# Swin attention and a spiking layer on one core: keys stored with the four column positions innermost, and ACT's norm of a row split around q's copy

## The reference

```python
x = x + window_attention(group_norm(x))   # 8x8 windows, 16 heads of 16 channels
x = x + spikes(group_norm(x) @ W.T + b)   # 8 samples are the 8 time steps

qkv  = part @ qkv_w.T + qkv_b             # part: 128 windows of 64 tokens
attn = softmax(q * 16**-0.5 @ k.T + bias[h] + MASK[window])
out  = attn @ v
# spikes: v = v + (x_t - v) / 2; s = v >= 1; v = v * (1 - s)
```

## Time and profile before

| | us |
|---|---|
| median of 3 runs | 545.47 |
| lowest, highest | 545.28, 548.49 |
| the profiled execution | 546.64 |
| its span, first to last instruction | 544.9 |
| PE busy | 434.2 (80%) |
| DVE busy | 398.2 (73%) |
| ACT busy | 377.4 (69%) |
| POOL busy | 280.3 (51%) |

### The profile page before, as it was taken

How to read it: one execution, slowest core, us unless ns; L and a number is a source line. 1 busy time by engine, 2 the same in 40 slices (tenths; PEclk the granted TensorE clock), 3 DMA queues, 4 the chain that set the end, 5 groups by cost and what they waited for, 6 DMA issues and landing times.

```text
span 544.9 us, 20474 instructions
## 1 busy us (share of the span) xinstructions
PE 434.2 (80%) x7912; PEld 403.4 (74%) x7912; DVE 398.2 (73%) x838; ACT 377.4 (69%) x863; POOL 280.3 (51%) x382
## 2 busy tenths in 40 slices
PE   0056658889878986988698879889988887889997
PEld 0056558878868886978698779778888776778886
DVE  5753757777776877677767767778877676588897
ACT  2353657878886887678778867788888786756551
POOL 6163456556654766475647654765685556640000
PEclk9996979999998999899989988999999998899999
DMA  7232534556554555455545654565555453023333
GB/s 204 67 81 65 140 75 107 142 142 155 138 139 109 141 138 137 109 128 142 138 114 133 139 131 112 129 140 134 123 118 119 111 125 80 2 78 136 135 137 135
DMA packets 155272, 65.78 MB, mean 121 GB/s; under 512 B 124978, under 2 KB 142644, under 8 KB 155188
## 3 DMA queue, kind: packets, MB, share of 16 engines
q1 hardware_dynamic: 154272, 64.52, 46.4%
q10 hardware_dynamic: 916, 0.01, 0.1%
HBM read 39.33 MB, written 25.17 MB: 118 GB/s over the span
## 4 chain that ended last, share of the span: by engine, by line
PE 38%; SPq 21%; ACT 11%; DMA 10%; issue 9%; DVE 8%; ACTq 1%; POOL 0%; DVEq 0%; POOLq 0%
SPq L317 12%; SPq L311 7%; DMA k_stack<-k_spill0lo 4%; PE pv_ps L1050 4%; PE proj_ps L939 3%; DMA k_stack<-k_spill1lo 3%; PE proj_ps L940 3%; PE proj_ps L941 3%; PE score_ps L1026 3%; PE score_ps L1016 3%; PE proj_ps L926 3%; PE pv_ps L926 3%; PE score_ps L926 3%; ACT xn L493 2%; ACT v_hi L529 2%
## 5 line engine op out<-in xcount | busy, mean ns | idle before, releaser
L454 POOL TENSOR_TENSOR p_lo<-probs,p_hi 128x512 f16<-128x512 f32 x128 | 146.4, 1165 | 147.3 <-ACT p_hi L608 122.9
L1016 PE MATMUL score_ps<-q_stack,k_stack 96*128 96x64 f16 x1024 | 88.1, 197 | 50.5 <-ACT max_rows L598 39.2
L1016 PEld LDWEIGHTS score_ps<-q_stack,k_stack 96*128 96x128 f16 x1024 | 74.2, 100 | 56.8 <-ACT max_rows L598 47.7
L785 DVE TENSOR_REDUCE neg_max<-max_ps 128x16 f16<-128x1024 f32 x64 | 78.4, 1225 | 42.9 <-PE max_ps L996 41.3
L607 ACT ACTIVATE probs<-score_ps 128x512 f32<-128x512 f32 x128 | 76.9, 601 | 38.4 <-PE score_ps L1026 37.6
L779 DVE TENSOR_TENSOR v_lo<-proj_ps,v_hi 64x256 f16<-64x256 f32 x128 | 54.2, 423 | 59.3 <-ACT v_hi L529 58.4
L939 PE MATMUL proj_ps<-xn_hi,w_hi 128*128 128x256 f32 x256 | 76.8, 300 | 10.7 <-DVE w_lo L738 7.2
L1012 PE MATMUL score_ps<-both_parts,bias_k 128*128 128x64 f16 x1024 | 80.8, 197 | 0.0
L608 ACT ACTIVATE p_hi<-score_ps 128x512 f16<-128x512 f32 x128 | 77.3, 604 | 0.0
L1012 PEld LDWEIGHTS score_ps<-both_parts,bias_k 128*128 128x128 f16 x1024 | 72.8, 100 | 2.8
L940 PE MATMUL proj_ps<-xn_lo,w_hi 128*128 128x256 f32 x256 | 73.8, 288 | 0.0
(11 more groups left out here) (131 smaller groups left out, 1211.4 us busy)
## 6 DMA issues: line engine op xcount, KB each, us to landing
xc<-in_x_dram SPq DMA_DIRECT2D x32, 256.0 KB, 3.1
out_dram<-xc SPq DMA_DIRECT2D x32, 256.0 KB, 2.2
q_stack<-q_spill0hi SPq DMA_DIRECT2D x32, 128.0 KB, 2.6
k_stack<-k_spill0hi SPq DMA_DIRECT2D x64, 64.0 KB, 3.5
q_stack<-q_spill1hi SPq DMA_DIRECT2D x32, 128.0 KB, 2.6
k_stack<-k_spill1hi SPq DMA_DIRECT2D x64, 64.0 KB, 3.4
q_spill0hi<-q_flat SPq DMA_DIRECT2D x16, 128.0 KB, 2.4
k_spill0hi<-k_flat SPq DMA_DIRECT2D x16, 128.0 KB, 1.9
```

Source lines behind the costliest of these rows:

```text
L454: pool.tensor_tensor(p_lo[p][:, quads, :, :].rearrange("p g w i -> p (g w i)"), probs[:, quads, :, :].rearrange("p g w i -> p (g w i)"), p ...
L785: dve.tensor_reduce(neg_max[:, :].rearrange("p (m n) -> p m n", m=2)[:, :, 0:8], max_ps[:, :, :].rearrange("p m (n j) -> p m n j", j=WS), ...
L1016: pe.matmul(dst, k_stack[slot][0:96, 2 * mid + q, at, :], q_stack[slot][0:96, 2 * mid + q, at, :], start=False, stop=False)
```

## The change

Four things change together. The key stack's tile gets the four column positions innermost: `[128, QUADS, HALVES, 128, WCOLS]` instead of `[128, QUADS, HALVES * WCOLS, 128]`. ACT and DVE write k_flat in that order already (token j, then window w), so they step 8 bytes from one f16 to the next while they read proj_ps in order. The reading back then moves pieces of 64 x 4 x 2 = 512 bytes instead of 64 x 2 = 128, with the same bytes and as many DMAs. PE reads the keys of one window with a step of 4 f16, 8 bytes, as weights in L1016 and as the moving operand in L996. On ACT the two instructions of `normalise` leave the end of the second pair: the first now stands ahead of `q_high`, the second between `q_high` and `k_high`.

```diff
-        k_stack = [sb(f"k_stack{i}", [128, QUADS, HALVES * WCOLS, 128], f16) for i in range(2)]
+        k_stack = [sb(f"k_stack{i}", [128, QUADS, HALVES, 128, WCOLS], f16) for i in range(2)]
...
+        def keys_of(buf, part):
+
+            if buf is k_flat:
+                return buf[:, part, :].rearrange("p (h j w) -> p h w j", h=HALVES, w=WCOLS)
+            return buf[:, part, :].rearrange("p (h w j) -> p h w j", h=HALVES, w=WCOLS)
...
-                    sp.dma_start(k_stack[slot][rows, quads, :, e * WS:(e + 1) * WS],
-                                 k_spill[slot][part][e * D:(e + 1) * D, quads, :].rearrange("d g (n j) -> d (g n) j", j=WS))\
+                    sp.dma_start(k_stack[slot][rows, quads, :, e * WS:(e + 1) * WS, :].rearrange("r g h j w -> r (g h) (j w)"),
+                                 k_spill[slot][part][e * D:(e + 1) * D, quads, :].rearrange("d g (h n) -> d (g h) n", h=HALVES))\
...
+            def normalise(row, sample, slot, norm, done, halves=range(HALVES)):
+
+                if 0 in halves:
+                    wait(act, xn_lo_done, done - 1)
+                last = normed(xn[slot], row, sample, norm, halves)
+                if HALVES - 1 in halves:
+                    last.then_inc(xn_done, 1)
...
-                act.activation(k_flat[:, 0, :], proj_ps[:, 1, :], ACT.Copy).then_inc(k_hi_done, 1)
+                act.activation(keys_of(k_flat, 0), keys_of(proj_ps, 1), ACT.Copy).then_inc(k_hi_done, 1)
...
-                if p == 1 and not is_last_row(row, 2):
-                    q_high(row + 3)
-                    k_high(row + 3)
+                if p == 1:
+                    sample = s + (k // 2 + 3) // WROWS
+                    for h in range(HALVES):
+                        if not is_last_row(row, 3):
+                            normalise(row + 3, sample, nxt % 2, sample + 1, row + 3, (h,))
+                        if not is_last_row(row, 2):
+                            (q_high, k_high)[h](row + 3)
...
-                if p == 1 and not is_last_row(row, 3):
-                    sample = s + (k // 2 + 3) // WROWS
-                    normalise(row + 3, sample, nxt % 2, sample + 1, row + 3)
...
-                dve.tensor_tensor(k_flat[:, 1, :], proj_ps[:, 1, :], k_flat[:, 0, :], ALU.subtract).then_inc(k_lo_done, 1)
+                dve.tensor_tensor(keys_of(k_flat, 1), keys_of(proj_ps, 1), keys_of(k_flat, 0), ALU.subtract).then_inc(k_lo_done, 1)
...
-                                                 k_stack[slot][rows, 2 * mid + q, at, :],
+                                                 k_stack[slot][rows, 2 * mid + q, h, :, 2 * (k % 2) + w],
...
-                                pe.matmul(dst, k_stack[slot][0:96, 2 * mid + q, at, :], q_stack[slot][0:96, 2 * mid + q, at, :],
+                                pe.matmul(dst, k_stack[slot][0:96, 2 * mid + q, h, :, 2 * p + w], q_stack[slot][0:96, 2 * mid + q, at, :],
```

9 lines of the change are left out of this document (3 added, 6 removed).

## The result

The kernel after took 590.62 us (median of 4 runs, 588.45 to 594.7), and before on the same chip 546.98 us (4 runs): a ratio of 1.080, with an interval from 1.070 to 1.089. The forecast was 547.8 us in a range up to 565. The profiled execution took 592.43 us, its span 590.7 us.

A forecast was written before the change was run, and what follows sets the result against it. PE and ACT alternate within a row of 12.27 us, with key transfers intruding now and then. Losses of 43.0 us less gains of 40.7 us, net +2.3 us, gave 547.8 us, in a range of 538 to 565 us.

The forecast's parts named there:

- the norm's gain: ACT's xn instructions leave the end of second pairs: 24 places of 1.13 us, 27.1 us gained.
- 512-byte pieces and their stacks: Key transfers in 512-byte pieces: 10.6 us of waits gained, and 2.0 us at the start.
- PE's step: 8-byte step in PE's key reads, weights of L1016 and moving operand of L996: taken as 0, far bound 100 us.
- strided copies: ACT's and DVE's copies of k write with an 8-byte step: taken as 0 more, 17 us at twice the time.
- norm moved in the pair k = 3, with the clock: ACT's norm waits for POOL's shift in samples 0 to 6: 32.0 us lost, plus 10 us for PE's low clock.
- rival 3: ACT pays for the strided write of k: 565 us, chance 0.07.
- the transfers' loop: From one lo spill of k to the next on SP: 12.8 us, expected to fall to 9 to 10 us.
- The issue of k's stacks: SP's issue of a full key transfer falls from 0.63 to 0.36 us; eight issues from 4.7 to 2.8 us.
- Rival 5: SP's issue doesn't shrink, the 12.8 us loop holds undisturbed rows, norm waits come on top: 588 us, chance 0.03.
- rival 2: PE pays for the 8-byte step at L1016, 49 ns a load, 50 us in all: 598 us, chance 0.09.
- The seven waits for POOL's shift: ACT's xn in the pair k = 3 waits seven times, about 5 us each, some 34 us in all.
- The two halves of the norm in ACT's idle time: In second pairs, around q's copy on ACT: no cost while the norm's input is there, k's copy no later.

The follow-up runs named there:

- contiguous copies: The changed kernel with the norm back behind the exponentials and k copied in plain order by ACT and DVE, keys of windows mixed: 544.53 us, ratio 0.992.
- PE's step alone: The kernel before with only PE's reads of k_stack stepping 8 bytes from key to key, over the same stored data: 550.51 us, ratio 1.010.
- layout alone: The changed kernel with both halves of the norm put back behind the exponentials: 563.26 us, ratio 1.026.
- norm alone where ready: The kernel before with the norm split around q's copy except in the pair k = 3, keys stored as before: 554.7 us, ratio 1.011.
- after, norm where ready: The changed kernel with the norm put back behind the exponentials in the pair k = 3 alone: 556.67 us, ratio 1.018.
- copies turned, norm where ready: The changed kernel with the norm put back at k = 3 and k's copies writing k_flat in its own order, reading the bank with the step: 536.44 us, ratio 0.977.

## Why the prediction was wrong

The runs split the loss in steps that the prediction had as terms. Each difference is between two kernels that differ in that step alone, in per cent of before times 5.47 us. The doubt is worked out from the intervals of the two ratios. The steps form one chain from before to after, so their sum is the whole by construction. I had counted 24 places of the norm's gain, 27.1 us; seven of them are the pairs k = 3, so here 17 x 1.13 = 19.2 us stand in the norm's row, and 42 - 7 x 1.13 = 34.1 in the row of k = 3:

| step | measured as | measured | doubt | predicted |
|---|---|---|---|---|
| 512-byte pieces and their stacks | contiguous copies (0.9921) less PE's step alone (1.0104) | -10.0 | 4.3 | -12.6 |
| PE's step | 1.0104 less 1 | +5.7 | 3.7 | 0 |
| strided copies | layout alone (1.0256) less contiguous copies (0.9921) | +18.3 | 3.4 | 0 |
| norm moved where ready | 1.0177 less layout alone (1.0256) | -4.3 | 5.8 | -19.2 |
| norm moved in the pair k = 3, with the clock | after (1.0796) less 1.0177 | +33.9 | 7.3 | +34.1 |
| sum | | +43.6 | 5.1 | +2.3 |

The 41.3 us between the sums are 18.3 us for the strided copies, 14.9 for the norm's gain, 5.7 for PE's step and 2.6 for the pieces; the largest single term, the pair k = 3, came out as forecast.

The distances between neighbouring pairs, in us from one trace each, show where these lie:

| stretches | before | layout alone | contiguous copies | norm alone where ready | after, norm where ready | after | copies turned, norm where ready |
|---|---|---|---|---|---|---|---|
| first to second, 19 | 125.1 | 135.2 | 123.8 | 135.0 | 140.2 | 140.7 | 127.8 |
| k = 2 to 3, 6 | 41.8 | 43.3 | 40.2 | 47.1 | 46.5 | 72.1 | 42.9 |
| second to first, 16 | 93.9 | 94.8 | 94.9 | 78.0 | 80.1 | 80.2 | 80.0 |
| k = 3 to 4, 6 | 35.1 | 35.2 | 35.2 | 36.6 | 35.2 | 40.3 | 35.2 |
| loop's turn, 4 | 35.9 | 40.0 | 38.6 | 41.3 | 38.3 | 38.1 | 36.8 |

**Strided copies: the step that failed first.** I took 0 and named the condition: at twice the time, 17 us, rival 3. The time was 2.2 times. The price of both copies was 18 us in the layout alone, 22 us with the norm moved where it is ready, and 27 us in before's layout. I had no row of a copy that writes with such a step, and put the value at the harmless end of an unknown range. The bound was near and the choice wrong. It had a second effect that I left out: I counted DVE's copy as hidden beside the scores, but the low part of k hangs on it, and its stack is the one that PE waits for. In before's layout the strided copies took the waits for k_stack from 10.6 to 23.9 us, in the new one from 2.6 to 4.9, and from 10.8 to 14.2 with the norm moved where it is ready. So the larger part of after's 16.1 us comes with the norm's move, and a smaller part from the copies.

**The norm's gain: mis-sized, 19.2 against 4.3 us.** The interval of the 4.3 takes in 0; in no kernel did the move give more than 10 us, and in before's layout it cost 6. Per place it was right: in the 16 stretches from a second to a first pair the norm alone takes 15.9 us, 1.0 us each, against 1.13. In the kernels with PE's step it is 0.9 us (94.8 to 80.1), presumably since PE is late next. What was wrong is the place where the gain ends: the transfers' loop, 12.8 us in the kernel before, is longer than the new row, and the first to second stretches pay back 9.9 us (125.1 to 135.0) in before's layout and 5.0 us (135.2 to 140.2) with the strided copies. And I had this loop down to 9 or 10 us by a cheaper issue, which didn't come.

**The issue of k's stacks: mis-sized, 0.36 to 0.60 us.** I drew a line through 0.63 us at 512 pieces and 0.45 us at 256, which were issues of one row, four of them full and two with half the quads. In before's trace the two half ones, equal in pieces, take 617 and 448 ns in the median, and the first of the full ones 549, so the number of pieces was never what set the difference: the 0.45 was read from the last of the six alone. The gain from the pieces is in the landing, 3.5 to 2.6 us. It came to 10.0 us against 12.6, close by luck, since the cause that carried most of the term did not act. Rival 5, with its 588 us, took the issue as unchanged and came out close to the measured time, but by another way: it had the transfers' loop hold the undisturbed rows at 12.8 us, and no strided copies in it. The undisturbed row of after takes 12.21 us, with max_rows behind the long copy, and k = 3 (33.9 us) and the copies (18.3) make more than the whole loss of 43.6. What rival 5 names is seen in the norm alone where ready, with 31.1 us of waits for the stacks in before's transfers.

**PE's step: 0 taken, 5.7 us measured.** I had asked only for the price of a load. The loads' median rose by 15 ns (98 to 113), five times the 3 ns from which rival 2 was to decide, and its 50 us did not come; nor did the 75 ns a matmul by which the moving operand slowed, 16 times a pair, of which, with the loads, 0.1 us a pair reach the end. How the 5.7 us divide between the two sides no run shows.

**What held.** The seven waits for POOL's shift: 36.8 us measured, about 34 forecast. Their cost with the clock, at the same places: 33.9 us against 34.1. Its two parts were less exact: by the table of distances the stretch into k = 3 got 4.3 us longer (4.9 forecast) and the one behind it 0.85 us (0.4 forecast, 1.5 of the clock less 1.13 of the norm). The two halves of the norm in ACT's idle time: no cost ahead of k's copy. The clock at its lower level behind 4.9 us of idle PE: 0.50 in the slice. The wait's cost and the clock's were not taken apart by a run; their sum alone is shown. In before's layout the same move at k = 3 cost 22.9 us (1.0524 less 1.0105), less than 33.9, though the intervals nearly meet; rows there were waiting for transfers already, which may be the reason and was not tested.

On the rule quoted in the prediction: the Trainium skill, page "SBUF — State Buffer", section "Door 1: The DMA port swizzle", says that accesses keep their full rate when at least two fall into each line of 16 bytes; by that a step of 8 bytes is just free. The traces disagree for this chip's copies and matmuls: written with that step by ACT, 1327 ns instead of 597; read as a moving operand, 291 ns instead of 216.

**Open.** DVE's copy got rid of a strided write and a strided read of SBUF at once, so which of the two it pays for isn't known; for ACT it is the write. What shorter issues on SP would bring by themselves is open too.

## What to carry to other kernels

When a layout change puts a step into an engine's access, look on which side it falls. Here ACT's copy took 1327 ns when it wrote f16 to SBUF with a step of 8 bytes and 597 ns when it read fp32 from PSUM with a step of 256 bytes instead; DVE's, which also read one operand from SBUF with the 8 bytes, took 1307 and 689 ns. So looping in the order of the destination gave the new layout for nothing: 4.1% or 22 us by swapping two letters.

An instruction moved ahead in an engine's queue is free only in those iterations where its input is there; one second pair in four cost here 34 us, three times the 10 us that the other three gave at best. Ask of each iteration of the unrolled schedule who writes the input and when, and move it in the others alone.

A gain on the engine that ends last is worth what the next loop allows: list the next one (here spill, issues, landing, last tile) before counting, and multiply only by the places that it leaves. Where a cost has no row in the trace and the path runs through it, don't put it at nothing: the copies' bad end was nearly the truth, while that of PE's step, 100 us, was far from the 5.7 measured. Here a run with that access alone told which.

## What was unexpected

- One transfer of 256 KB, 8 KB a partition, landed in 5.0 to 5.8 us as the last of a row, two of 64 KB each in 3.2 us (128-byte pieces) or 2.6 (512-byte pieces). Fewer and larger pieces helped here only while the bytes stayed the same.
- The duration of an issue on SP hardly depends on the pieces: 626 ns in the median in before, where a full one has 512 pieces, and 598 in after, where it has 128.
- A load of weights took 98 ns at 2 bytes from element to element and 113 at 8, a matmul of 128 f16 columns 216 and 291, one of 256 fp32 columns 279 and, with 256 bytes between columns, 305 (medians).
